# Second cross attention, selection stage: order of the work at its begin and at its end

## The reference

```python
Q = (x_text @ Wq).reshape(Bb, Tt, H, DH)            # H = 4 heads of 32, on the layer-normed x
K = (x_vision @ Wk).reshape(Bb, Gg, H, DH)          # 4096 keys a batch
scores = jnp.einsum('bthd,bghd->bhtg', Q, K) / np.sqrt(DH)
scores = jnp.where(vision_mask[:, None, None, :], scores, -jnp.inf)
topv, topi = jax.lax.top_k(scores, K_TOP)            # K_TOP = 32
probs = jax.nn.softmax(topv, axis=-1)
attn = jnp.zeros_like(scores).at[bi, hi, ti, topi].set(probs)
attn_mean = attn.mean(axis=1)                        # over the 4 heads
c_t = jnp.einsum('btg,bgd->btd', attn_mean, x_vision @ Wv) * text_mask[..., None]
x = layernorm(x_text, g_norm_in, b_norm_in)          # scaled and shifted by c_t @ W_film_in
y = s4d(x, ...)                                      # long convolution, by Fourier matrices
...                                                  # second film, feed-forward, norms
```

## Time and profile before

| | |
|---|---|
| median of 3 runs | 2303.34 us (2302.92 to 2304.7) |
| the profiled execution | 2318.84 us |
| its span, first to last instruction | 2317.0 us |
| busy, share of the span | PE 81%, DVE 53%, ACT 44%, POOL 32% |
| the stage `stage_x1a` | about 1247.6 to 1910.5 us of the span |

### The profile page before, as it was taken

How to read it: one execution, slowest core, us unless ns; L and a number is a source line. 1 busy time by engine, 2 the same in 40 slices (tenths; PEclk the granted TensorE clock), 3 DMA queues, 4 the chain that set the end, 5 groups by cost and what they waited for, 6 DMA issues and landing times.

```text
span 2317.0 us, 34831 instructions
## 1 busy us (share of the span) xinstructions
PE 1866.9 (81%) x13676; PEld 1137.7 (49%) x13676; DVE 1237.4 (53%) x3075; ACT 1026.6 (44%) x1381; POOL 746.1 (32%) x665
## 2 busy tenths in 40 slices
PE   5879998999999998886778787786868657976675
PEld 2434544454455445564565244454544445765553
DVE  5142332424232202635882768979868956536575
ACT  1357567656756782221311434545444420113452
POOL 6244234414333400000200356777748601110000
PEclk7989999999999998999787556687776778988887
DMA  6656457664655520001100021221311322000000
GB/s 139 127 101 122 100 122 120 118 128 93 121 111 111 85 70 1 2 1 60 61 1 13 1 62 39 61 79 44 92 49 48 103 72 108 1 1 1 1 5 14
DMA packets 78046, 150.01 MB, mean 65 GB/s; under 512 B 15464, under 2 KB 63144, under 8 KB 71464
## 3 DMA queue, kind: packets, MB, share of 16 engines
q1 hardware_dynamic: 64304, 101.80, 15.7%
q0 software_dynamic: 12768, 42.59, 12.1%
q10 hardware_dynamic: 792, 3.17, 0.4%
HBM read 93.59 MB, written 2.62 MB: 42 GB/s over the span
## 4 chain that ended last, share of the span: by engine, by line
PE 52%; DVE 22%; ACT 12%; issue 6%; POOL 4%; DMA 3%; DVEq 0%; ACTq 0%; POOLq 0%; SPq 0%
PE R L112 33%; PE B L112 17%; ACT P L571 7%; DVE PM L1700 5%; DVE CA L1658 4%; PE B L178 2%; POOL KST L789 2%; ACT PM L1585 2%; DVE CA L1670 1%; DVE T L1672 1%; ACT PS L2266 1%; DMA KST<-OV 1%; POOL ACC L1773 1%; ACT RT L116 1%; DMA CT<-in_ctxT 1%
## 5 line engine op out<-in xcount | busy, mean ns | idle before, releaser
L571 ACT ACTIVATE P<-R 128x1024 f32<-128x1024 f32 x512 | 507.1, 1026 | 220.8 <-PE R L112 185.0
L112 PE MATMUL R<-QS,KST 100*128 100x256 bf16 x2048 | 297.5, 277 | 63.7 <-ACT P L571 53.2
L112 PEld LDWEIGHTS R<-QS,KST 100*128 100x128 bf16 x2048 | 170.5, 98 | 228.3 <-ACT P L571 121.0
L116 ACT ACTIVATE SC<-R 128x1024 f32<-128x1024 f32 x128 | 129.5, 1023 | 256.4 <-PE R L112 143.5
L1658 DVE MAX8 CA<-SC 128x8 f32<-128x128 f32 x1024 | 203.2, 276 | 15.7 <-ACT SC L116 14.8
L200 POOL TENSOR_TENSOR LNrs<-LNve,pk_const 128x2 f32<-128x2 f32 x36 | 25.3, 703 | 535.2 <-DVE LNve L196 535.0
L112 PE MATMUL R<-OV,QT 32*128 32x512 f32 x512 | 197.3, 860 | 0.0
L1773 POOL TENSOR_TENSOR ACC<-ACC,PM 128x4096 f32<-128x4096 f32 x21 | 186.1, 8862 | 1.8
L1700 DVE SCALAR_TENSOR_TENSOR PM<-SC,T,PM 128x4096 f32<-128x4096 f32 x32 | 147.9, 4658 | 50.8 <-ACT AT L116 33.3
L789 POOL DMA_DIRECT2D KST<-OV x300 | 144.5, 490 | 70.8 <-PE R L112 53.9
L112 PE MATMUL R<-P,VP 128*32 128x256 f32 x2304 | 155.9, 387 | 0.7 <-ACT P L571 0.3
(11 more groups left out here) (360 smaller groups left out, 3356.9 us busy)
## 6 DMA issues: line engine op xcount, KB each, us to landing
KST<-OV POOLq DMA_DIRECT2D x276, 128.0 KB, 11.1
CT<-in_ctxP SPq DMA_DIRECT2D x40, 768.0 KB, 4.9
CN<-in_ctxn SPq DMA_DIRECT2D x64, 384.0 KB, 3.3
CT<-in_ctxT SPq DMA_DIRECT2D x64, 192.0 KB, 2.4
KST<-OV SPq DMA_DIRECT2D x84, 128.0 KB, 10.2
KST<-in_ctxP ACTq DMA_DIRECT2D x4, 768.0 KB, 9.5
QS<-x_q POOLq DMA_DIRECT2D x24, 128.0 KB, 5.4
pk_a<-in_pk_a SPq DMA_DIRECT2D x1, 3014.0 KB, 16.9
```

Of the source, the lines that this page charges most:

```text
L112: return e.matmul(o, l, r, start=st, stop=sp, skip_group_check=True)
L116: return e.activation(o, i, ACT.Copy)
L571: e.activation(P[(32 * p + k0) % 3][:, :], ring.at(("s", p, k0))[:, :], ACT.Exp).then_inc(*EX.up((p, k0)))
```

## The change

At the start of `stage_x1a`, VectorE makes the statistics of batch 0 alone, GpSimd takes its root, and `q_norm(0)` and the mask follow; the text mask's cast and the other three batches' statistics stand behind them. ScalarE's exponential of block 0, head 0 moves from behind the 8 copies of block 1 to behind the fifth. At the end of the stage the addition of block 14, head 1 goes to GpSimd; VectorE adds block 15 alone, in two halves of 2048 keys, both reciprocals first, and the transposes of m = 7 wait for their own half. The load of `x1c` moves from the start of `stage_x1b` to step 17 of `stage_x1a`, into the buffer of the even blocks' scores (now `S0`, which outlives the stage), and ScalarE's wait for it moves behind its first copies.

```diff
@@ stage_x1a @@
-            SC = [sbt(c, f"SC{i}", [128, 2, NK]) for i in range(2)]
+            SC = [two(S0[:, :]), sbt(c, "SC1", [128, 2, NK])[:, :, :]]
...
-                return p == NP - 1 or p == NP - 2 and h == 1
+                return p == NP - 1
...
-                    if g == 0:
-                        e.wait_ge(*summed(2 * m + 1))
+                    if g % 4 == 0:
+                        e.wait_ge(*summed(2 * m + 1, g // 4))
...
+                        if n == 1 and ch == 4:
+                            weigh(0, 0)
-                    if 0 <= n - 1 < NP:
+                    if 1 <= n - 1 < NP:
                         weigh(n - 1, 0)
...
+                def add():
+                    p = NP - 1
+                    sm, acc = SM[p % 3], ACC[1]
+                    for h in range(2):
+                        rc = sm[:, h, REC:REC + 1]
+                        e.wait_ge(*V.at(("sel", p, h)))
+                        e.tensor_scalar(rc, sm[:, h, SUM:SUM + 1], 4.0, None, ALU.mult).then_inc(*V.up())
+                        e.wait_ge(*V.now())
+                        e.reciprocal(rc, rc).then_inc(*V.up())
+                    e.wait_ge(*G.at(("sum", p - 1, 1)))
+                    for k in range(2):
+                        part = slice(k * NK // 2, (k + 1) * NK // 2)
+                        for h in range(2):
+                            e.wait_ge(*V.now())
+                            e.scalar_tensor_tensor(acc[:, part], PM[(2 * p + h) % 3][:, part], sm[:, h, REC:REC + 1], acc[:, part], ALU.mult, ALU.add).then_inc(*V.up(("sum", p, h, k)))
...
+                stats(0, 0, 2)
+                e.memset(ON1[:, :], 1.0).then_inc(*QV.up())
+                e.memset(ONB[:, :], 1.0).then_inc(*QV.up("ones"))
+                q_norm(0)
+                mask(0)
                 e.wait_ge(*LM1.at("m1"))
                 e.tensor_copy(M1F[:, :], M1U[:, :]).then_inc(*QV.up("m1"))
...
+                stats(1, 2, 2 * NB)
...
                         load(e, "x1b", OV[:, 0:spec["x1b"][0]], LB)
+                    if n == NP + 1:
+                        e.wait_ge(*V.at(("sel", NP - 2, 1)))
+                        load(e, "x1c", t_x1c, LC1)
@@ stage_x1b @@
             def scalar(e):
-                e.wait_ge(*LC1.at("x1c"))
...
                     elif s == 8:
+                        if b == 0:
+                            e.wait_ge(*LC1.at("x1c"))
...
             def sync(e):
-                load(e, "x1c", t_x1c, LC1)
```

More of the change, by code:

```diff
@@ L1415, in stage_moe, with stage_x1a @@
             return dict(tensor=tensor, vector=vector, scalar=scalar, gpsimd=gpsimd, sync=sync, slots=(ring, bank))
-        def stage_x1a(c, x1a):
+        def stage_x1a(c, x1a, S0, t_x1c):
             w = x1a[1]
@@ L1471, in by_vector, with summed @@
             def by_vector(p, h):
-                return p == NP - 1 or p == NP - 2 and h == 1
-            def summed(p):
-                return (V if by_vector(p, 1) else G).at(("sum", p, 1))
+                return p == NP - 1
+            def summed(p, k):
+                return V.at(("sum", p, 1, k)) if by_vector(p, 1) else G.at(("sum", p, 1))
             def tensor(e):
@@ L1582, in weigh @@
                     if i >= 3:
-                        e.wait_ge(*(V if by_vector(*divmod(i - 3, 2)) else G).at(("sum", *divmod(i - 3, 2))))
+                        e.wait_ge(*G.at(("sum", *divmod(i - 3, 2))))
                     e.wait_ge(*V.at(("nm", p, h)))
@@ L1639, in q_norm @@
                         e.wait_ge(*M.at(("xt", b - 1)))
-                    else:
-                        e.wait_ge(*G.at("rs"))
+                    e.wait_ge(*G.at(("rs", min(b, 1))))
                     for k in range(2):
@@ new lines, in stats @@
+                def stats(n, a0, a1):
+                    for a in range(a0, a1):
+                        e.bn_stats(BST[:, a, :], X[:, a, :]).then_inc(*QV.up())
+                    e.wait_ge(*QV.now())
+                    for a in range(a0, a1):
+                        e.bn_aggr(MV[:, a, :], BST[:, a, :]).then_inc(*QV.up())
+                    e.wait_ge(*QV.now())
+                    e.tensor_scalar(RSD[:, a0:a1], MV[:, a0:a1, 1], 1e-5, None, ALU.add).then_inc(*QV.up(("ve", n)))
+                stats(0, 0, 2)
@@ L1742, in vector @@
                             top(n - 1, h)
[L1743 to L1747, removed]
+                    if n == NP + 1:
+                        add()
             def gpsimd(e):
                 e.memset(NG1[:, :], -1.0).then_inc(*GI.up())
-                e.wait_ge(*QV.at("ve"))
-                e.tensor_tensor(RSD[:, :], RSD[:, :], cst["nhalf"][:, 0:1].broadcast_to([128, 2 * NB]), ALU.pow).then_inc(*G.up("rs"))
+                for n, a0, a1 in ((0, 0, 2), (1, 2, 2 * NB)):
+                    e.wait_ge(*QV.at(("ve", n)))
+                    e.tensor_tensor(RSD[:, a0:a1], RSD[:, a0:a1], cst["nhalf"][:, 0:1].broadcast_to([128, a1 - a0]), ALU.pow).then_inc(*G.up(("rs", n)))
                 for p in range(NP):
@@ L1812, in sync, with stage_x1b @@
                         load(e, "x1b", OV[:, 0:spec["x1b"][0]], LB)
+                    if n == NP + 1:
+                        e.wait_ge(*V.at(("sel", NP - 2, 1)))
+                        load(e, "x1c", t_x1c, LC1)
             return dict(tensor=tensor, vector=vector, scalar=scalar, gpsimd=gpsimd, sync=sync, slots=(ring, bank))
-        def stage_x1b(c, late):
+        def stage_x1b(c, late, w2):
             w = dict(pack(c, "x1b", OV)[1])
-            t_x1c, w2 = pack(c, "x1c")
             w.update(w2)
@@ L1827, in stage_x1b @@
                     nb[nm, i] = sbt(c, f"{nm}{i}", sh)[:, :, :]
-            M, V, S, G, LC1 = sig("x1b_product"), sig("x1b_vector"), sig("x1b_copy"), sig("x1b_pool"), dsig("w_x1c")
+            M, V, S, G = sig("x1b_product"), sig("x1b_vector"), sig("x1b_copy"), sig("x1b_pool")
             order = woven([14] * NB)
@@ L2498, in build @@
         KM1, KC1, KLD = sig("x1_key_product"), sig("x1_key_copy"), dsig("kernel")
+        LC1 = dsig("w_x1c")
         CT1 = [dsig(f"x1_ct{i}") for i in range(2)]
@@ L2510, in build @@
         CS = sbt(ctx, "CS", [128, 2 * NB, 192])
+        S0 = sbt(ctx, "S0", [128, 2 * NK])
+        t_x1c, x1c = pack(ctx, "x1c", S0)
         with ExitStack() as c:
-            stages.append(stage_x1a(c, x1a))
+            stages.append(stage_x1a(c, x1a, S0, t_x1c))
         late = {nm: pack(ctx, nm) for nm in ("a1", "qf")}
         with ExitStack() as c:
-            stages.append(stage_x1b(c, late))
+            stages.append(stage_x1b(c, late, x1c))
         with ExitStack() as c:
```

## The result

The changed kernel took 2289.68 us in its first comparison (median of 4 runs, 2286.03 to 2301.4), against 2303.24 us before: a ratio of 0.9938 with a 95% interval of 0.991 to 0.9966, so 14 us faster. Forecast were 2279 us, with 2273 to 2287 as the range. The direction was right; the time lay outside. Two later comparisons of the same kernel gave 0.9895 and 0.9896: 24 us, the forecast's size. Why both can be is the subject of what follows.

What follows compares the result with a forecast made beforehand. At three places one engine works while the others wait, so shortening those chains shortens the kernel: 5.6 + 1.85 + 6.8 + 10.2 = 24.5 us, scaled to 24.3, from 2303.3 to 2279.0 us; 2273 to 2287 held 8 in 10.

Steps and rivals of the forecast that it cites:

- Part 1 and 2: Start of selection: batch 0 normed first, 5.6 us; block 0's first exponential behind the fifth copy, 1.85 us.
- The mask row: Start of selection: its loads might land late and hold up the scores; at most 1 us of loss allowed.
- Part 3: End of selection: block 14's addition on GpSimd and block 15 in halves start the last sum 6.8 us earlier.
- the term for the context load: First load of m = 7, behind `x1c`, lands 11.4 us after its issue; first product waits about 2 us.
- The 0.7 us taken off there for the smaller pack: Landing behind `x1c`: about 0.7 us less because `x1c` is 250 KB smaller than `x1b`.
- Part 4: Begin of next stage: `x1c` loaded earlier ends the waits for it, 10.2 us; 6.1 if the clock stays low.
- The clock stayed up: Next stage: without the 6.81 us pause, `c2` of both batches runs at 2.4 GHz; rival of low clock 15%.
- both gains shift the whole loop of 16 blocks: Selection loop: nothing is tied to an absolute time, so the start's 7.4 us arrive whole at step 16.
- The prediction's own sign of being wrong: Selection loop: the forecast is wrong if the blocks' period changes between step 3 and step 15.
- absorbed: Rival, 8%: the start's 7.4 us are lost in the loop by an unseen wait, giving 2286 us.
- 2% rival on a whole stage at 0.50: Rival, 2%: the shifted loop meets TensorE's clock worse, at 0.50 from 1400 to 1840, giving 2317 us.

Runs made afterwards that it cites:

- e12: Changed kernel with the load of `x1c` issued behind the first two context loads of m = 7 instead of ahead; ratio 0.9916 to the kernel before.
- e11: Kernel before with only the new end of the selection (block 14's last addition on GpSimd, block 15 in halves); ratio 0.9954 to the kernel before.
- e2: Changed kernel with the old start (all statistics first, both exponentials of block 0 behind the copies); ratio 0.9933 to the kernel before.
- e5: Changed kernel with two extra 128-row products per chunk of scores, their result overwritten; ratio 1.005 to the kernel before.
- e6: Kernel before with two extra 128-row products per chunk of scores, their result overwritten; ratio 1.0197 to the kernel before.
- e7: Changed kernel with one extra 128-row product per chunk of scores, its result overwritten; ratio 0.9993 to the kernel before.
- e13: Kernel before with half of the selection's context products left out, so sums lack half of their keys; ratio 1.0084 to the kernel before.
- e14: Changed kernel with half of the selection's context products left out, so sums lack half of their keys; ratio 0.9981 to the kernel before.
- e3: Changed kernel with only the early exponential of block 0 undone; ratio 0.9934 to the kernel before.
- e4: Kernel before with only the new start (batch 0's norm first, early exponential of block 0); ratio 0.999 to the kernel before.
- e1_again: The changed kernel, unedited, timed again against the kernel before; ratio 0.9895.

## Why the prediction was right and where it failed

*Part 1 and 2* (5.6 and 1.85 us): right. The segment to the first select is 7.57 us shorter; undoing the exponential alone returns 2.05, so 5.5 are the norm's. The mask row didn't hold the scores up: their first product starts 0.06 us behind ScalarE's copy of the queries, at 1251.62.

*Part 3* (6.8): 7.9 in the profile, 8.4 and 8.5 in the repeats. The mechanism was right, the term for the context load mostly too pessimistic: it was forecast to be waited for about 2 us, and was for 0.51, 0.24 and 0.28 in the three profiles of the changed kernel. `x1c` was issued 6.7 us behind the flag product and not 8.0, since TensorE's products of m = 6 ran more at 2.4 GHz, and the first load of m = 7 landed 11.1 us behind it, where 11.4 was forecast. (The 0.7 us taken off there for the smaller pack should be 0.9 by the prediction's own rows.) e12 and e11 put the price of that order at 0.5 to 1.6 us; in e2, with `x1c` issued 7.1 us behind the flag product, the wait was 1.73 and the end 3.4 us longer than in e11.

*Part 4* (10.2): 10.6 in the first pair, and 27.4 us in every kernel that has it; since the old order took 35.3 to 39.1, the gain is 8 to 12 from execution to execution. The clock stayed up where the 6.81 us pause was gone, as forecast; e11, which keeps the pause, keeps a first `c2` of 3.78 us. Behind the first XR the changed kernel took 370.4 to 371.0 us in its profiles and before 368.4, so up to 2 us may come back there; no run follows them up.

*The step that failed* is "both gains shift the whole loop of 16 blocks ... so 7.4 us should arrive at step 16", and the range built on it. What the runs showed in its place is a loop of 565.5 us instead of 555.4: it took back 10 us, more than the 7.4 that should have passed through it. The argument that nothing in the loop is tied to an absolute time is true and not enough: it makes the loop's time independent of when it starts, not constant. I read the loop's 555 us from one execution, two of whose blocks took 37 and 39 us, as if it were a property of the program. Over 11 profiles of these programs (all but e5, e6, e7, e13 and e14) it is 543.5 to 565.5 us. The prediction's own sign of being wrong came true in step 6, with a period of 39.0 instead of 33.4. My only allowance was 8% for "absorbed", and the clock I had only as a 2% rival on a whole stage at 0.50, where it comes in single blocks of 5 to 6 us. That rival also priced it only once TensorE alone fills the stretch; in fact a block is 6 us longer while TensorE is busy 31.55 of 39.03 us. With that scatter in the sum the range had to be some 10 us to either side, an estimate from the 22 us between the shortest and the longest loop. That the two later comparisons fell on the forecast's ratio is in part luck: a loop as in the first profile lies outside.

*Open* is whether the new start also makes long blocks more frequent. The six profiles with it have loops of 545.2 to 565.5 us, the five without 543.5 to 555.4; the new start alone gained 2.3 us instead of 7.6, and the block from 13 to 14 was long in all three profiles of the changed kernel and in none with the old start, though in none of e3, e4 and e12 either. Against that stand the two later comparisons (24 us, where the segments sum to 26) and e13 beside e14 (22 to 24). A loss of some us on the mean fits all of them, and so the cause of the first comparison's missing 10 us is shown as to its mechanism, long blocks at the lower level, but not as to how much of it was chance.

## What to carry to other kernels

A gain ahead of a long loop is measured with the loop's scatter on top, and the loop may keep a part of it: read each part in its own segment of several profiles, and take the time from many runs. Before treating a loop's span as fixed, list the periods of its iterations; if some are longer with the same work on every other engine, look at TensorE's granted clock there. A late load moved forward paid twice here, because it also removed a TensorE pause; it cost least behind the small loads that are needed first (e12).

## What the runs showed of the hardware

In the first scores TensorE was busy 39.52 of 40 us, and the granted clock stayed at 0.50; 102 of the 115 records are products of 1 and 32 rows. Two more products of 128 rows a chunk did not change that at this place in e5 (40.00 us busy, 0.50) and did a little in e6 (40.00 us, 0.62). In the loop, taking half of the context products (128 rows) away lowered the clock from 0.69 to 0.53 (e14) and from 0.71 to 0.60 (e13), and the whole kernel became 0.86% of before, 20 us, longer than the same program with them (e14 and e1_again, each against before on its own chip); adding many 128-row products raised it only to 0.77 and 0.79. The Trainium skill (TensorE: Matmul & The Clock Gate, Part 1) says that activity releases the throttle. If that is measured by the profile's busy time, these runs don't agree: TensorE was busier in e14 (361.6 of 440 us at 0.53) than in the changed kernel (345.0 at 0.69).

A load of 384 KB issued behind one of about 2.7 MB in the same queue took 8.2 us to land instead of 3.3, and a select that met a GpSimd addition 7.6 us instead of 4.49.
